# Mixture stage: a 256-row ninth routed pass with an expert chosen by register

## The reference

```
top1 = argmax(softmax(xf @ gate_w.T))                # one of 2 routed experts per token
h = relu(einsum('end,edh->enh', masked_by(top1), w1) + b1[:, None, :])
expert_out = einsum('enh,ehd->end', h, w2) + b2[:, None, :]
shared = relu(xf @ sw1 + sb1) @ sw2 + sb2            # every token
x = x + 0.5 * (expert_out.sum(axis=0) + shared)      # hidden size 1024
```

## Time and profile before

| what | value |
|---|---|
| median of 3 runs | 3241.82 us (3233.46 to 3247.18) |
| profiled execution, its own time | 3211.57 us |
| span of the profile | 3209.6 us, mean granted TensorE clock 0.972 |
| matmuls of mixture stage a, first to last start | 6.4 to 434.0 us |
| the same of stage b | 768.0 to 1174.6 us from its first pass on |
| ninth routed pass of stage a, `up` of its step 0 to `up` of pass 14 | 338.99 to 362.28 us |

### The profile page before, as it was taken

One profiled execution on the slowest core, in us unless ns is written; L12 is line 12 of the kernel. 1 busy time (PEld: TensorE's weight loads), 2 busy tenths in 40 slices (PEclk: granted clock), 3 DMA queues, 4 the chain that ended last, 5 costly groups with the idle time before them and its releaser, 6 DMA issues. The chain is left out here.

```text
span 3209.6 us, 62375 instructions
## 1 busy us (share of the span) xinstructions
PE 3039.3 (95%) x24516; PEld 2019.9 (63%) x24516; DVE 2457.1 (77%) x4826; ACT 2058.9 (64%) x3764; POOL 555.1 (17%) x612
## 2 busy tenths in 40 slices
PE   7999979987999979987999999999999999997998
PEld 6899968776989969984343333334333333343998
DVE  7533468875533389984988999999999999983987
ACT  5544534444644546652577888887888888876665
POOL 3322235543412242220000000000000000001222
PEclk9999989998999989997799999999999999998999
DMA  4211120002211110003303012020303030000000
GB/s 128 85 44 36 50 70 2 2 2 61 94 40 42 35 43 1 1 1 94 41 28 49 20 19 25 12 31 2 42 2 42 2 42 2 2 2 1 14 18 23
DMA packets 60962, 100.45 MB, mean 31 GB/s; under 512 B 7632, under 2 KB 44160, under 8 KB 57984
## 3 DMA queue, kind: packets, MB, share of 16 engines
q1 hardware_dynamic: 54144, 78.62, 11.3%
q0 software_dynamic: 6528, 17.83, 1.8%
HBM read 65.36 MB, written 30.93 MB: 30 GB/s over the span
## 5 line engine op out<-in xcount | busy, mean ns | idle before, releaser
L2258 DVE TENSOR_REDUCE smxp<-psum 128x1 f32<-128x512 f32 x2048 | 1258.6, 681 | 39.8 <-PE psum L2109 38.4
L2218 ACT ACTIVATE spr<-psum 128x512 f32<-128x512 f32 x2048 | 1113.9, 596 | 266.9 <-PE psum L2133 219.4
L2109 PE MATMUL psum<-sks,sqs 48*128 48x512 f32 x2048 | 783.3, 463 | 12.4 <-DMA sqs<-q_parts 11.6
L2133 PE MATMUL psum<-sqs,sks 50*128 50x512 f32 x2048 | 752.7, 452 | 0.0
L2150 PE MATMUL psum<-spr,sv 128*32 128x256 f32 x8192 | 657.0, 392 | 11.3 <-ACT sot L2225 8.7
L2109 PEld LDWEIGHTS psum<-sks,sqs 48*128 48x128 f32 x2048 | 322.0, 189 | 432.8 <-issue 382.4
L2150 PEld LDWEIGHTS psum<-spr,sv 128*32 128x32 f32 x8192 | 162.8, 108 | 380.9 <-ACT spr L2218 293.7
L2133 PEld LDWEIGHTS psum<-sqs,sks 50*128 50x128 f32 x2048 | 301.8, 185 | 16.0 <-issue 9.3
L1835 POOL MEMSET fhqb<- 128x64 f32 x3 | 0.3, 152 | 1498.4 <-POOLq L2022 1498.4
L526 PE MATMUL psum<-w_a,hsa_hi 128*128 128x256 f32 (+1 forms) x1088 | 198.3, 281 | 1.4 <-DVE hsa_lo L776 1.4
L526 PE MATMUL psum<-w_b,hsb_hi 128*128 128x256 f32 (+1 forms) x1088 | 197.1, 279 | 0.3 <-DVE hsb_lo L776 0.3
(11 more groups left out here) (413 smaller groups left out, 5942.1 us busy)
## 6 DMA issues: line engine op xcount, KB each, us to landing
sks<-q_parts SPq DMA_DIRECT2D x42, 256.0 KB, 9.1
sqs<-q_parts SPq DMA_DIRECT2D x42, 256.0 KB, 19.7
q_parts<-spart SPq DMA_DIRECT2D x16, 512.0 KB, 2.9
f_routed_a<-yoa SPq DMA_DIRECT2D x9, 512.0 KB, 2.9
f_routed_b<-yob SPq DMA_DIRECT2D x9, 512.0 KB, 2.9
x<-in_L_attn_x_dram SPq DMA_DIRECT2D x8, 512.0 KB, 7.2
yoa<-in_L_ffn_w_dram SPq DMA_DIRECT2D x16, 256.0 KB, 2.8
xga<-f_sorted_a SPq DMA_DIRECT2D x8, 512.0 KB, 3.8
```

Of the source, the lines that this page charges most:

```text
L2109: e.matmul(bank(what), QS[n % 2][rows, pr, q0:q0 + P], KS[n % 2][rows, pr, jc * GW:(jc + 1) * GW], start=True, stop=True, tile_position=(H ...
L2133: e.matmul(out, KS[n % 2][rows, pr, jt * P:(jt + 1) * P], QS[n % 2][rows, pr, ic * GW:(ic + 1) * GW], start=True, stop=True, tile_position ...
L2218: e.activation(PR[j % 2][:, HEAD[i], :], src, ACT.Exp, scale=float(DH) ** -0.5).then_inc(*done.up)
L2258: e.tensor_reduce(out[:, r // (2 * GT * IC), r // (2 * IC) % GT, r // 2 % IC, r % 2:r % 2 + 1], bank(what), AX.X, ALU.max).then_inc(*pm_fr ...
```

## The change

The group with the border is now cut at its middle. It goes through the expert of its majority half: `expert[r]` compares the middle of group r (second row of `limit`, based at `HW` = 256) with the number of first-expert rows. The 256-row half that holds the border goes once more, through the other expert, in the ninth pass, which has 256 rows. Which expert that is depends on the data, so `expert` has nine entries, POOL copies weights and bias for the ninth pass too, and `down` and `finish` read by register there as well. `low` (the first row of that half) and `odd` (its expert) are worked out in `routes`. Gathers of mixed rows: 2 instead of 4. Transposes, evacuation and `low_x` of the ninth pass: one of two. `up` there: 6 matmuls of 256 columns; `down`: 6 matmuls of 256 columns; `hidden` and `low`: 256 columns; `finish`: one operation instead of two; the result written by SP: 256 rows. Semaphore counts of transposes and results go through `pairs(p)`. Both stages, a and b, have the change.

```diff
@@ -275,6 +275,9 @@
+XP = SF + G
+HX = GT // 2
+HW = HX * P
@@ -310,9 +313,9 @@
-table_i = sb(f"table_i_{tag}", [P, T + G + GT], I32, scope)
-table = sb(f"table_{tag}", [P, T + G + GT], scope=scope)
-place_of, limit, row_of = table[:, 0:T], table[:, T:T + G], table[:, T + G:T + G + GT]
+table_i = sb(f"table_i_{tag}", [P, T + 2 * G + HX], I32, scope)
+table = sb(f"table_{tag}", [P, T + 2 * G + HX], scope=scope)
+place_of, limit, row_of = table[:, 0:T], table[:, T:T + 2 * G], table[:, T + 2 * G:T + 2 * G + HX]
@@ -325,13 +328,13 @@
-cut = sb(f"cut_{tag}", [P, 4], scope=scope)
-below = sb(f"below_{tag}", [P, G], scope=scope)
-expert = sb(f"expert_{tag}", [P, G], I32, scope)
-mixed_i = sb(f"mixed_i_{tag}", [P, GT], U32, scope)
+cut = sb(f"cut_{tag}", [P, 7], scope=scope)
+below = sb(f"below_{tag}", [P, 2, G], scope=scope)
+expert = sb(f"expert_{tag}", [P, NR], I32, scope)
+mixed_i = sb(f"mixed_i_{tag}", [P, HX], U32, scope)
...
-routed_y = nc.dram_tensor(f"f0_routed_{tag}", [NR * GW, D], F32).ap()
+routed_y = nc.dram_tensor(f"f0_routed_{tag}", [T * P + HW, D], F32).ap()
@@ -357,6 +360,18 @@
+def pairs(p):
...
+    return 2 * p - (p > XP)
...
+def pairs_of(p):
...
+    return 1 if p == XP else 2
...
+def width(p):
...
+    return GW // 2 * pairs_of(p)
@@ -366,7 +381,7 @@
-    return mixed_in(GT) if r == G else xs_in[(SF + r) % 2](r // 2 + 1)
+    return mixed_in(HX) if r == G else xs_in[(SF + r) % 2](r // 2 + 1)
@@ -456,9 +471,10 @@
-            e.wait_ge(*done(2 * (SF + r + 1)))
-            e.dma_start(routed_y[r * GW:(r + 1) * GW, :].rearrange("(t p) d -> p t d", p=P),
-                        YO[r % 2][:]).then_inc(*y_out[r % 2].up)
+            e.wait_ge(*done(pairs(SF + r + 1)))
+            n = width(SF + r)
+            e.dma_start(routed_y[r * GW:r * GW + n, :].rearrange("(t p) d -> p t d", p=P),
+                        YO[r % 2][:, 0:n // P, :]).then_inc(*y_out[r % 2].up)
@@ -471,7 +487,7 @@
-            n, slot = 2 * p + i, p % 2
+            n, slot = pairs(p) + i, p % 2
@@ -495,18 +511,18 @@
-                e.wait_ge(*xlo(2 * p + 2))
+                e.wait_ge(*xlo(pairs(p + 1)))
...
-            if r is not None and r < G:
+            if r is not None:
...
-                w = [w1[:, v, 0 if r is None else NE - 1, :, c * P:(c + 1) * P] for v in range(2)]
+                w = [w1[:, v, 0, :, c * P:(c + 1) * P] for v in range(2)]
...
-                    m = e.matmul(psum[:, n % 3, :], w[u][:, k, :], XT[p % 2][v][:, k, :],
+                    m = e.matmul(psum[:, n % 3, 0:width(p)], w[u][:, k, :], XT[p % 2][v][:, k, 0:width(p)],
@@ -519,9 +535,9 @@
-                e.wait_ge(*done(2 * (p - 1)))
-            ex = 0 if r is None else NE - 1 if r == G else 1 + chosen[r]
-            for i in range(GT):
+                e.wait_ge(*done(pairs(p - 1)))
+            ex = 0 if r is None else 1 + chosen[r]
+            for i in range(width(p) // P):
@@ -581,7 +597,7 @@
-            if p + 1 < PASSES and c in turn_steps(p):
+            if p + 1 < PASSES and c in turn_steps(p)[:pairs_of(p + 1)]:
@@ -589,7 +605,7 @@
-            n = p * 2 + i
+            n = pairs(p) + i
@@ -605,10 +621,9 @@
+            cols = slice(0, width(p))
...
-            if r == G:
-                bias = b1[:, NE - 1, c:c + 1]
-            elif r is not None:
+            if r is not None:
@@ -617,8 +632,8 @@
-            e.activation(hi[:], psum[:, n % 3, :], ACT.Relu, bias=bias)
-            e.activation(hid[:], psum[:, n % 3, :], ACT.Relu, bias=bias).then_inc(*hid_ok.up)
+            e.activation(hi[:, cols], psum[:, n % 3, cols], ACT.Relu, bias=bias)
+            e.activation(hid[:, cols], psum[:, n % 3, cols], ACT.Relu, bias=bias).then_inc(*hid_ok.up)
@@ -639,7 +654,7 @@
-                e.wait_ge(*xturn(2 * (p - 2) + 2))
+                e.wait_ge(*xturn(pairs(p - 1)))
@@ -682,7 +697,7 @@
-                if c - 1 in turn_steps(p):
+                if c - 1 in turn_steps(p)[:pairs_of(p + 1)]:
@@ -746,22 +761,29 @@
-            q, high, more = cut[:, 0:1], cut[:, 1:2], cut[:, 2:3]
-            e.tensor_scalar(expert[:], limit, nfirst[:, 0:1], None, ALU.is_ge).then_inc(*dv.up())
-            small(e.tensor_scalar(below[:], limit, nfirst[:, 0:1], None, ALU.is_le))
-            small(e.tensor_reduce(cut[:, 3:4], below[:], AX.X, ALU.add))
-            e.tensor_scalar(high, cut[:, 3:4], float(GW), None, ALU.mult).then_inc(*dv.up())
-            e.tensor_scalar(q, cut[:, 3:4], float(GW), float(-GW), ALU.mult, ALU.add).then_inc(*dv.up())
-            small(e.tensor_scalar(more, cut[:, 3:4], float(-GW), float(T * P + GW), ALU.mult, ALU.add))
-            e.tensor_scalar(mixed_i[:], row_of, q, None, ALU.add).then_inc(*dv.up())
-            small(e.tensor_scalar(back[:], pos[:], high, more, ALU.is_lt, ALU.mult))
-            small(e.tensor_tensor(back[:], back[:], second[:], ALU.mult))
+            low, high, more, count = (cut[:, i:i + 1] for i in range(4))
+            halves, odd = cut[:, 4:6], cut[:, 6:7]
+            e.tensor_scalar(expert[:, 0:G], limit[:, G:2 * G], nfirst[:, 0:1], None, ALU.is_gt).then_inc(*dv.up())
+            small(e.tensor_scalar(below[:].rearrange("p a g -> p (a g)"), limit, nfirst[:, 0:1], None, ALU.is_le))
+            small(e.tensor_reduce(halves, below[:], AX.X, ALU.add))
+            e.tensor_scalar(odd, halves[:, 1:2], halves[:, 0:1], 1.0, ALU.subtract, ALU.add).then_inc(*dv.up())
+            e.tensor_scalar(expert[:, G:NR], halves[:, 1:2], halves[:, 0:1], 1.0, ALU.subtract, ALU.add).then_inc(*dv.up())
+            small(e.tensor_tensor(count, halves[:, 1:2], halves[:, 0:1], ALU.add))
+            e.tensor_scalar(high, count, float(HW), None, ALU.mult).then_inc(*dv.up())
+            e.tensor_scalar(low, count, float(HW), float(-HW), ALU.mult, ALU.add).then_inc(*dv.up())
+            small(e.tensor_scalar(more, count, float(-HW), float(T * P + HW), ALU.mult, ALU.add))
+            e.tensor_scalar(mixed_i[:], row_of, low, None, ALU.add).then_inc(*dv.up())
+            small(e.tensor_scalar(back[:], pos[:], low, more, ALU.is_ge, ALU.mult))
+            small(e.scalar_tensor_tensor(out=back[:], in0=pos[:], scalar=high, in1=back[:], op0=ALU.is_lt,
+                                         op1=ALU.mult))
+            small(e.scalar_tensor_tensor(out=back[:], in0=second[:], scalar=odd, in1=back[:], op0=ALU.is_equal,
+                                         op1=ALU.mult))
...
-            e.wait_ge(*xhi(p * 2 + i + 1))
+            e.wait_ge(*xhi(pairs(p) + i + 1))
@@ -773,7 +795,8 @@
-            e.tensor_tensor(lo[:], HB[n % 2][:], hi[:].bitcast(F32),
+            cols = slice(0, width(n // C0))
+            e.tensor_tensor(lo[:, cols], HB[n % 2][:, cols], hi[:, cols].bitcast(F32),
@@ -790,12 +813,11 @@
-            for j in range(GT // 2):
+            for j in range(pairs_of(p)):
...
-                    ex = 1 if r == G else chosen[r]
...
-                                    other[:, ex, :].unsqueeze(1).to_broadcast([P, 2, D]),
+                                    other[:, chosen[r], :].unsqueeze(1).to_broadcast([P, 2, D]),
@@ -803,7 +825,7 @@
-                        e.wait_ge(*done(2 * p + j + 1))
+                        e.wait_ge(*done(pairs(p) + j + 1))
@@ -821,7 +843,7 @@
-                e.wait_ge(*done(2 * (t // GT if t // GT < SF else t // GT + NR) + 2))
+                e.wait_ge(*done(pairs((t // GT if t // GT < SF else t // GT + NR) + 1)))
@@ -849,7 +871,7 @@
-        e.wait_ge(*table_ok(NB + 3))
+        e.wait_ge(*table_ok(NB + 4))
@@ -937,7 +959,7 @@
-                if r == G - 2 and c % 2:
+                if r == G - 2 and c % 2 and c // 2 < HX:
@@ -959,8 +981,10 @@
-        e.iota(table_i[:, T:T + G], pattern=[[GW, G]], base=0, channel_multiplier=0).then_inc(*table_ok.up)
-        e.iota(table_i[:, T + G:], pattern=[[P, GT]], base=0, channel_multiplier=1).then_inc(*table_ok.up)
+        for a in range(2):
+            e.iota(table_i[:, T + a * G:T + (a + 1) * G], pattern=[[GW, G]], base=a * HW,
+                   channel_multiplier=0).then_inc(*table_ok.up)
+        e.iota(table_i[:, T + 2 * G:], pattern=[[P, HX]], base=0, channel_multiplier=1).then_inc(*table_ok.up)
@@ -974,7 +998,7 @@
-        for r in range(G):
+        for r in range(NR):
```

More of the change, by code:

```diff
@@ L992, in ffn0 @@
                 b2_ok.close(3)
-                table_ok.close(NB + 3)
+                table_ok.close(NB + 4)
                 consts_ok.close(2)
@@ L999, in ffn0 @@
                 xn_ok.close(T)
-                xturn.close(2 * PASSES)
-                xhi.close(2 * PASSES)
-                xlo.close(2 * PASSES)
+                xturn.close(pairs(PASSES))
+                xhi.close(pairs(PASSES))
+                xlo.close(pairs(PASSES))
                 if tag == "a":
@@ L1021, in ffn0 @@
                 down_ok.close(END)
-                done.close(2 * PASSES)
-                bias_ok.close(G)
-                copied.close(G * C0)
+                done.close(pairs(PASSES))
+                bias_ok.close(NR)
```

(1 more changed line is left out.)

2 lines of the change are left out of this document (1 added, 1 removed).

## The result

In the first comparison, of four runs each, the changed kernel took 3205.14 us (median; 3199.51 to 3210.18) and the kernel before 3238.60 us (3233.46 to 3247.18): ratio 0.9897 [0.987, 0.9923], 33.5 us less. The forecast was 22.1 us less, 3219.7 us, and the range ended at 3207. The direction was right, the size was not: of the 14.6 us between 3219.7 and 3205.14, 11.4 are gain that was not forecast, and 3.2 come from the kernel before, whose median fell from 3241.82 to 3238.60 us with its fourth run. Of the runs further on, one of register_only_r2 took 4095 us and one of the kernel before beside it 9393 us; the ratios leave both out.

What follows compares the result with a forecast made beforehand. PE's stream of matmuls was taken to bound the changed place. Removed work of 11.6 us less a 0.5 us stall gave 11.1 us a stage, 22.1 for both: 3241.82 - 22.1 = 3219.7 us, range 3207 to 3233.

Steps and rivals of the forecast that it cites:

- Costs of the removed work: PE, per stage: 5.6 us from `up`, 5.6 from `down`, 0.36 from one set of transposes; together 11.6 us.
- the forecast 13.8: Ninth pass, from its first `up` to that of pass 14: 13.8 us, with short steps of 1.40 us.
- second price of the matmul terms: Ninth pass `up` and `down`: 5.1 and 5.2 us by the page's N/2.4 + 2.5 ns; the trace's rows were kept instead.
- Stalls and additions: PE waits 0.5 us a stage at the second transposes; `routes` 0.7 us more but hidden; copies and ninth register cost nothing.
- A: Short steps limited by ACT (up to 3 us a stage) or PE's instruction stream (1.9 us): 3228 us; chance 0.13.
- B: Clock falls in the ninth pass, 213 instead of 117 ns a matmul, costing 9.2 us a stage: 3238 us; chance 0.07.
- C: Low clock outlasts the ninth pass; low through passes 14 to 16 it gives 3350 us, slower; chance 0.03.
- D: Work shorter but not the stage, something unseen pacing passes 13 to 16: 3242 us; chance 0.05.
- The step that failed: Whole kernel: the 22.1 us gain taken off the median 3241.82 us, 30 us above the profiled execution.
- the term for passes 14 to 16 and their add-back gathers: From `finish` of pass 13 on, add-back and gathers move along with full steps: no gain or loss.
- 3 us either way for the spread of medians: Whole kernel: allowance for measurement scatter within the forecast's own range of 3210 to 3226 us.
- its own range for the forecast: Whole kernel: 3210 to 3226 us, from no stall to 3 us a stage, with 3 us either way; chance 0.72.

Runs made afterwards that it cites:

- register_only_r2: Repeat: kernel before with 512 rows kept, ninth expert (always the second) through a register and weight copies; 3212.39 us, ratio 0.9989.
- The fixed-address kernel: Changed kernel with its 256-row ninth pass always through the second expert at fixed addresses, no weight copies; 3189.59 us, ratio 0.9931 to the kernel before.
- before_r2: Kernel before, unchanged, run and profiled again; 3235.6 us, ratio 1.0006 to the kernel before beside it.
- session 2: One-chip session timing both kernels unchanged and both without add-back gathers, beside the kernel before at 3234.89 us.
- after_r2: Changed kernel, unchanged, run and profiled again; 3202.54 us, ratio 0.9893 to the kernel before.
- before_shift_r3: Kernel before with 16 already satisfied waits added to ACT's stream in passes 11 and 12, third run; 3238.77 us, ratio 1.0006.
- half_only_r4: Fourth run of the changed kernel with its ninth pass always through the second expert, fixed addresses, no copies; 3205.88 us, ratio 0.9907 to the kernel before.
- session 5: One-chip session timing the fixed-address short pass (ratio 0.9907) and the kernel before with 16 extra ACT waits (1.0006), beside the kernel before at 3235.21 us.
- half_only: Changed kernel, ninth pass of 256 rows always through the second expert at fixed addresses, no weight copies; 3189.59 us, ratio 0.9931 to the kernel before.

## Why the prediction was right in its place and short in its total

**Costs of the removed work: right.** Per stage, 185.4 + 23.29 + 17.7 us became 184.9 + 14.25 + 16.3: 10.9 us less, where 11.6 - 0.5 = 11.1 were forecast. This is the same in every profile of either kernel, at both levels. The ninth pass is 0.42 us longer than the forecast 13.8: short steps run at 1.43 to 1.51 us and not 1.40. The fixed-address kernel has most of that too (14.12). The prediction's second price of the matmul terms, 5.1 and 5.2 us by the formula of the Trainium skill ("TensorE: Matmul & The Clock Gate", section "Back-to-back issue gap"), uses what the page gives for an isolated matmul and not for a stream.

**Stalls and additions: right.** PE waits 0.31 us for 0.5, at the place named. `routes` takes 2.5 us against 1.7, 0.8 more for 0.7, and its timeline shows that nothing waits for it. Copies and register change no time that the runs can tell.

**The rivals fell.** A wanted ACT or the instruction stream to limit the short steps: of its 4.4 us a stage above the forecast some 0.4 is there. B and C wanted a lower clock: in the changed kernel it is 1.00 in the ninth pass (above) and through passes 14 to 16 (in before_r2 it is 0.79 from 404 to 412 us, behind a late start of ACT):

```profile
352.36:374.26 21.90, 21.90 (x142) 19.74 (x141) 8.91 (x17) 12.06 (x22) 9.38 (x10) 1.00 0.21 62
374.26:397.00 22.74, 21.27 (x139) 18.92 (x138) 18.46 (x50) 12.85 (x22) 12.22 (x13) 1.00 0.27 78
397.00:426.90 29.90, 28.05 (x184) 24.97 (x183) 21.61 (x57) 11.19 (x18) 9.47 (x10) 1.00 0.16 47
```

The Trainium skill ("TensorE: Matmul & The Clock Gate", table "Why this matters for your kernels") warns against thin matmul work that is neither contiguous nor padded, because of the clock; the prediction took from it the 9.2 us of rival B. The pass of 256 columns took 14.25 us at clock 1.00 with waits of at most 0.31 us: it was contiguous, which the same row allows, so this case neither bears the warning out nor refutes it. D fell as well: the ninth pass and what follows at the lower level are as short as the work.

**The step that failed** is this one: "That execution lies 30 us below the median of the runs; most of the span is other stages, so I take the same microseconds off the median". It took the 30 us for time that the change doesn't touch. With it failed the term for passes 14 to 16 and their add-back gathers, which the prediction put at nothing ("No gain or loss"): at the upper level the gathers cost the kernel before 11.3 us and the changed one 3.1 us (the estimate at one clock, session 2), and those 8.2 us are most of the gain that was missing. The profiled execution of before (3211.57 us, clock 0.972) was one of the lower level, the median (3241.82) one of the upper. For the lower level the forecast, 3211.57 - 22.1 = 3189.5 us, was met: 3193.96 and 3189.34 us. That the one profile of before was of the lower level, where no tail is late, was chance. And of the distance between the levels most lies in the mixture stages themselves, next to the change: from before's profile to that of before_r2, stage a grew from 415.5 to 425.8 us and stage b from 406.6 to 416.7, 20.4 us of a span longer by 22.6 (3232.2 - 3209.6). 9.0 of them are the first 32 steps, 10.7 the tails. A part of the 9.0 is clock: it is 0.97 and 0.98 over those steps of the two stages in before and 0.95 and 0.96 in before_r2.

Two smaller things in the prediction's chances don't hold. Its "3 us either way for the spread of medians" is too little: six medians of the kernel before lie between 3215.33 and 3238.60 us. And its own range for the forecast doesn't come out of its terms: no stall to 3 us a stage is a gain of 23.2 to 17.2 us, with 3 us either way 3215.6 to 3227.6 us, and not 3210 to 3226.

At the upper level the pair before_r2 and after_r2 shows where 32.4 us go, both stages together. Their spans differ by 24.8 us (3232.2 - 3207.4), the mixture stages by 26.5 (842.5 - 816.0): the columns of the change give 21.8, the tails 8.2 (118.7 - 110.5), and the first 32 steps give 3.3 back (209.9 against 213.2). These are single executions: another profile of the changed kernel (after, in the table) has tails of 58.3 and 58.2 us, hardly better than before's 59.9 and 58.8. Tails above their 54.0 us, by profiles at the upper level with gathers, are 5.9, 4.8, 4.4 and 3.0 us a stage for 512 rows (the latter two of before_shift_r3) and 4.3, 4.3, 2.1, 0.4, 2.1 and 4.7 for 256 rows (the last two of half_only_r4): means of 4.5 and 3.0.

**What stays open.** Shown is that add-back gathers cause late starts of ACT in passes 14 to 16 at the upper level only, and that without them the gain falls to that of the lower level. The theory with which the runs were planned, that ACT there waits for its own instructions to come, is not borne out: its wait had begun 5.6 us before and PE's signal ended it. The Trainium skill ("Runtime: NRT & Kernel Launch", section "Instruction fetch mechanics") says that this fetch is hidden behind the pace of issue; the trace agrees at the gaps of 4.67 and 5.95 us. Why the signal is late, and what indirect transfers have to do with it, no run shows. Nor is it shown why the changed kernel loses less: in session 2 its gathers cost 8.2 us less, but over all upper-level profiles the tails explain only some 3 us of gain (means of 4.5 and 3.0 us a stage), so that part of the 8.2 us may be the luck of few executions. Two candidates that ran were placement of code, which session 5 bounds at a few us, and the register part, which session 5 could not separate. What makes a level is unknown: it is not the clock (above), and one chip showed both.

No run points to a version better than the changed kernel: half_only is not told from it at either level, and isn't right for all data.

## What to carry to other kernels

Price removed matmuls by the distances of starts of the same form in the trace; that was right here to 0.2 us in 11. Before a gain read from one profile is taken off a median that lies elsewhere, find where the difference between the two lies: if it is in the stage that the change touches, the gain is not the same at both. And compare kernels only beside each other on one chip, in several sessions, and at the same granted clock: the same two kernels gave 21 to 27 us and 32 to 33.5 us by medians here, and 22.5 to 24.1 and 31.2 us at clock 0.970.
